# Twenty-six matmuls with unread results in two waits of TensorE

## The chip, the cores and the metric

The kernel runs on one core of one Trainium2 chip, in one launch. The metric is the device time in microseconds (us). The median of three runs before the change is 799.12 us.

## What is computed

Two layers on x of shape (4, 1024, 128), each with an attention part and a feed-forward part, all in float32. The change lies in the first layer, between the end of its attention and the start of its mixture of experts:

```python
x = x + _L0_attn_ref(_layernorm(x), Wq, bq, Wk, bk, Wv, bv, Wo, bo)   # 16 heads, causal, ALiBi
x = x + _L0_ffn_ref(_layernorm(x), Wr, br, W1, b1, W2, b2)           # 8 experts
x = x + _L1_attn_ref(_layernorm(x), Wq, Wk)                          # softmax(tanh(scores)) @ x
x = x + _L1_ffn_ref(_layernorm(x), weight, disha)
```

The feed-forward part of the first layer is a router and eight experts:

```python
logits = x @ Wr + br
gate = max(softmax(logits)); idx = argmax(logits)      # one expert per token
pos = cumsum(one_hot(idx)) over all 4096 tokens        # position in the expert's queue
gate = gate * (pos < 512)                              # each expert takes its first tokens only
out = gate * (relu((gate * x) @ W1[idx] + b1[idx]) @ W2[idx] + b2[idx])
```

## The kernel before

The program is two blocks. The first holds the attention of the first layer; its unnormalised weighted sums and the softmax denominators go to DRAM, and at its end the last batch of them is loaded back. The second block, `later_stages`, does the rest. It works on 32 tiles of 128 tokens, in 8 chunks of 4 tiles. Every engine has its own list of instructions, which it works off in the order in which the code writes them, and the engines meet at semaphores; there is no planner in this block.

TensorE's list in the second block begins with two products of weights into `psFold` (lines 1226 and 1227). Then `pe.wait_ge(rden_ready, B)` waits until VectorE has inverted the last denominators (line 1024), which wait for their DMA. `reciprocals(j)` (line 1195) spreads the inverted denominators of chunk j over the partitions, one matmul of 128x128 by 128x512 float. VectorE multiplies them with the weighted sums (`divide`, line 1030), TensorE multiplies with Wo (`project`, line 1203, 4 matmuls), and VectorE adds the result to the residual (`add`, line 1039) and takes statistics (line 1042). Two of the chunks are under way at a time. The layer norm ends in `apply` on VectorE (line 1066) or ScalarE (line 1353), and then TensorE transposes a chunk (`turned`, line 1215) and computes its logits (`logits`, line 1222, 4 matmuls of 8 columns).

Behind the last logits VectorE alone forms maximum, one-hot choice and, after three matmuls for counts (lines 1248 to 1250), positions and gates (lines 1111 to 1124). TensorE waits for the first gated chunk (`xg_ready`, line 1253), transposes it (`gated_columns`, line 1258), makes the one-hot rows (`one_hot_rows`, line 1264), with ScalarE's copies behind each (lines 1377, 1381, 1382). Then the loop over 8 chunks x 8 experts begins: `expert_in` (lines 1273 and 1274), ScalarE's Relu (line 1390), `expert_out` (line 1282), with the second layer's steps of earlier chunks set between them by a fixed table.

Every float matmul shows in the trace as two matmul records and two weight loads, a transpose as one of each.

PSUM areas that matter: `psLg` is half a bank pair, 512 columns, of which the logits of all tiles fill the first 256; `psT2[0]` holds the transposed chunks with even numbers, of which the last is read before the logits end. `ident` is the 128x128 identity, `sel` a 0/1 array of 128 x 8 x 128; both are constants in SBUF.

Of the kernel before, what the change touches and what calls it, by code (L numbers as in the profile page):

```python
# [19 lines left out]
CW = CH * P  # L20
# [861 lines left out]
def later_stages(nc, ctx, sb, sem, w, shared, out):  # L882

    x_res, ot, den, ident, half_pow, half, banks = (
        shared[k] for k in ("x_res", "ot", "den", "ident", "half_pow", "half", "banks"))
    wts_in, o_in, xb_ready, rden_ready, n_later, identb = (
        shared[k] for k in ("wts_in", "o_in", "xb_ready", "rden_ready", "n_later", "identb"))
    wo, wr, brb, rank, sel, incl, same, less = (
        w[k] for k in ("wo", "wr", "brb", "rank", "sel", "incl", "same", "less"))
# [56 lines left out]
    psRb, psProj, psT2, psLg = [half[0], half[1]], [banks[0], banks[1]], [half[2], banks[2]], half[3]  # L946
# [241 lines left out]
    def _(pe):  # L1188
        pe.wait_ge(wts_in, 16 * n_later)

        def reciprocals(j):

            if j >= 2:
                pe.wait_ge(at_ready, j - 1)
            nc.tensor.matmul(psRb[j % 2], sel[:, j, :], den[:, :, :].rearrange("p s q -> p (s q)"),
                             start=True, stop=True).then_inc(rb_psum, 1)
# [29 lines left out]
        nc.tensor.matmul(psFold[:, 0:P], w1q[:, :], w1k[:, :], start=True, stop=True)  # L1226
        nc.tensor.transpose(psFold[:, P:2 * P], wf[:, :], ident[:, :]).then_inc(fold_psum, 1)

        pe.wait_ge(rden_ready, B)
        reciprocals(0)  # L1230
        for j in range(CHUNKS):
# [16 lines left out]
        nc.tensor.matmul(psZ[0][:, 0:TILES * E], incl[:, :], flat, start=True, stop=True)  # L1248
        nc.tensor.matmul(psZ[0][:, TILES * E:2 * TILES * E], same[:, :], flat, start=True, stop=True)
        nc.tensor.matmul(psY[:, 0:TILES * E], less[:, :], flat, start=True, stop=True).then_inc(cnt_psum, 1)  # L1250

        def gated_columns(j):
            pe.wait_ge(xg_ready, j + 1)
            pe.wait_ge(fold_ready, 1)
            if j >= 1:
                pe.wait_ge(hott_ready, 2 * j)
            for i in range(CH):
                last = nc.tensor.transpose(psG[:, P * i:P * i + P], xg[:, j % 2, i, :], ident[:, :])
            last.then_inc(g_psum, 1)
# [34 lines left out]
        for n, (expert, due) in enumerate(slots()):  # L1294
            for name, j in due:
# [10 lines left out]
                if name == "s":  # L1306
                    pe.wait_ge(ut_ready, j + 1)
                    for i in range(CH):
                        last = nc.tensor.matmul(psS[:, P * i:P * i + P], xt3[:, P * i:P * i + P], ut[:, P * i:P * i + P],
                                                start=True, stop=True)  # L1310
                    last.then_inc(s_psum, 1)
                if name == "mix":
# [4 lines left out]
                    for i in range(CH):  # L1317
                        c0 = (i % 2) * (CW // 2)
                        last = nc.tensor.matmul(psMix[i // 2][:, c0:c0 + D + 1], ee[:, i, :], xe[:, j % 2, i, 0:D + 1],  # L1319
                                                start=True, stop=True)  # L1320
# [129 lines left out]
```

## Time and profile before

| | before |
|---|---|
| median of 3 runs | 799.12 us (798.9 to 801.77) |
| profiled execution, its own time | 797.04 us |
| its span, first to last instruction | 795.3 us |
| TensorE matmul busy | 662.6 us (83%) |
| VectorE busy | 515.1 us (65%) |
| ScalarE busy | 448.7 us (56%) |
| GpSimd busy | 153.8 us (19%) |
| mean granted TensorE clock | 0.921 of full |

The profile is of one execution. PE is TensorE's matmuls, PEld its weight loads, DVE VectorE, ACT ScalarE, POOL GpSimd. "L1195" is line 1195 of the kernel. The granted clock is 1.00 at 2.4 GHz and 0.50 at 1.2 GHz. A row of the timeline gives start, time, engine, line, operation, written and read tiles, shapes and count, and in brackets how long the engine had been idle and what released it.

### The profile page before, as it was taken

The numbers are of one execution on the slowest core, as the hardware profiler recorded it, in microseconds if no ns is written. First come the engines' busy times: TensorE is split into PE (matmuls) and PEld (weight loads), VectorE is DVE, ScalarE is ACT, GpSimd is POOL, SyncE is SP. The second block draws the span as 40 slices with busy tenths as digits, with TensorE's granted clock in tenths as the row PEclk, the third lists the DMA queues.
The fourth block names the chain that finished last, engine by engine and source line by source line (L and its number), as shares of the span: only waits on it lengthen the run. The fifth ranks groups of instructions, "written<-read, shape, count | busy, mean of one in ns | idle before, by whom it ended". The sixth has DMA issues, their size and how long they took to land.

```text
span 795.3 us, 14721 instructions
## 1 busy us (share of the span) xinstructions
PE 662.6 (83%) x5478; PEld 315.9 (40%) x5478; DVE 515.1 (65%) x1024; ACT 448.7 (56%) x765; POOL 153.8 (19%) x245
## 2 busy tenths in 40 slices
PE   3656988999989899889899885765799999999953
PEld 2431333333323233333333220455356666666643
DVE  5999788998888888889788830574221345333443
ACT  2950777788777887778777884032234443344310
POOL 2660122212221222212451221030000011010110
PEclk9995899999999999999999998685699999999965
DMA  6494645422212341332203000100000000000001
GB/s 157 133 200 122 160 109 139 107 46 49 52 34 48 72 76 36 75 72 50 50 7 77 6 10 10 28 1 0 1 0 1 10 6 14 14 14 6 9 13 27
DMA packets 49806, 40.58 MB, mean 51 GB/s; under 512 B 9772, under 2 KB 44724, under 8 KB 49724
## 3 DMA queue, kind: packets, MB, share of 16 engines
q1 hardware_dynamic: 43576, 37.22, 20.2%
q10 hardware_dynamic: 6160, 2.43, 1.3%
q8 instruction: 44, 0.72, 0.4%
q14 instruction: 26, 0.21, 0.1%
HBM read 22.32 MB, written 17.04 MB: 49 GB/s over the span
## 4 chain that ended last, share of the span: by engine, by line
PE 62%; DVE 19%; ACT 6%; issue 6%; POOL 3%; DMA 2%; SPq 0%; POOLq 0%; DVEq 0%; ACTq 0%
PE sums L756 15%; DVE neg_max L783 10%; PE ring L735 10%; PE ring L1282 9%; PE ring L1273 8%; PE bank L707 5%; ACT probs L804 5%; PE ring L1274 3%; PE bank L701 2%; DVE probs L506 2%; PE ring L1286 1%; PE bank L1319 1%; PE bank L1222 1%; PE bank L1330 1%; PE ring L718 1%
## 5 line engine op out<-in xcount | busy, mean ns | idle before, releaser
L783 DVE TENSOR_REDUCE neg_max<-bank 128x2 f32<-128x1024 f32 (+2 forms) x320 | 342.8, 1115 | 60.9 <-PE bank L707 58.8
L804 ACT ACTIVATE probs<-ring 128x512 f32<-128x512 f32 (+4 forms) x481 | 301.8, 681 | 79.8 <-PE ring L735 66.8
L735 PE MATMUL ring<-q_operand,k_operand 56*128 56x512 bf16 (+3 forms) x768 | 164.3, 333 | 18.2 <-ACT probs L804 14.5
L756 PE MATMUL sums<-probs,v_all 128*9 128x512 f32 (+3 forms) x1536 | 162.4, 495 | 2.7 <-POOL probs L837 2.1
L707 PE MATMUL bank<-k_operand,q_operand 54*128 54x512 bf16 (+3 forms) x768 | 144.5, 338 | 7.0 <-DVE v_all L514 5.3
L837 POOL TENSOR_SCALAR_AFFINE_SELECT probs<-probs 128x512 f32<-128x512 f32 x128 | 80.2, 635 | 215.6 <-ACT probs L804 214.7
L735 PEld LDWEIGHTS ring<-q_operand,k_operand 56*128 56x128 bf16 x768 | 50.2, 94 | 152.6 <-ACT probs L804 110.5
L1390 ACT ACTIVATE hid<-ring,b1c 128x512 f32<-128x512 f32 x64 | 44.0, 687 | 81.9 <-PE ring L1274 81.7
L701 PE MATMUL bank<-masks 64*128 64x128 bf16 (+2 forms) x768 | 71.9, 224 | 5.2 <-DVE neg_max L783 4.9
L1282 PE MATMUL ring<-w,hid 128*128 128x128 f32 x512 | 74.9, 290 | 0.0
L1273 PE MATMUL ring<-xgt,w 128*128 128x512 f32 x128 | 69.0, 621 | 1.2 <-ACT noth L1382 1.2
L1282 PEld LDWEIGHTS ring<-w,hid 128*128 128x128 f32 x512 | 62.8, 193 | 14.5 <-issue 12.9
L991 POOL TENSOR_TENSOR rs<-ve,half_pow 128x4 f32<-128x4 f32 x16 | 16.1, 1007 | 233.1 <-DVE ve L1011 233.1
L707 PEld LDWEIGHTS bank<-k_operand,q_operand 54*128 54x128 bf16 x768 | 46.1, 97 | 24.5 <-DVE neg_max L783 14.8
L701 PEld LDWEIGHTS bank<-masks 64*128 64x128 bf16 x768 | 36.7, 95 | 37.9 <-DVE neg_max L783 25.4
L1143 DVE SCALAR_TENSOR_TENSOR x_res<-ring,gate,x_res 128x128 f32<-128x128 f32 x32 | 9.0, 344 | 58.8 <-PE ring L1286 58.8
L756 PEld LDWEIGHTS sums<-probs,v_all 128*9 128x9 f32 x1536 | 23.2, 88 | 53.5 <-issue 39.8
L1179 DVE TENSOR_TENSOR res<-x_res,bank 128x512 f32<-128x512 f32 x8 | 5.5, 688 | 54.2 <-PE bank L1330 54.2
L718 PE MATMUL ring<-identb,max_parts 128*32 128x128 bf16 x32 | 7.1, 221 | 24.7 <-POOL max_parts L854 23.5
L1274 PEld LDWEIGHTS ring<-noth,big 8*128 8x128 bf16 x64 | 5.8, 91 | 50.0 <-issue 50.0
L1024 DVE RECIPROCAL denominators<-denominators 128x128 f32<-128x128 f32 x1 | 1.0, 952 | 37.3 <-DMA denominators<-weighted_sums 37.3
L1274 PE MATMUL ring<-noth,big 8*128 8x512 bf16 x64 | 25.1, 392 | 0.0
(156 smaller groups left out, 654.8 us busy)
## 6 DMA issues: line engine op xcount, KB each, us to landing
q_operand<-q_rows SPq DMA_DIRECT2D x64, 96.0 KB, 3.4
k_operand<-k_rows SPq DMA_DIRECT2D x32, 192.0 KB, 4.0
q_rows<-qk_parts SPq DMA_DIRECT2D x36, 128.0 KB, 2.4
k_rows<-qk_parts SPq DMA_DIRECT2D x36, 128.0 KB, 2.4
weighted_sums<-osum SPq DMA_DIRECT2D x128, 18.0 KB
sums_in<-in_L_attn_x SPq DMA_DIRECT2D x4, 512.0 KB, 7.3
q_operand<-max_rows_sb SPq DMA_DIRECT2D x128, 2.0 KB
sums_in<-weighted_sums SPq DMA_DIRECT2D x4, 512.0 KB
```

Of the source, the lines that this page charges most:

```text
L701: nc.tensor.matmul(ends, masks[rows, 0, a, :], masks[rows, 1, a:a + 1, 64 * a:P].to_broadcast([64, len(pairs), P - 64 * a]), start=a == 0, ...
L707: last = nc.tensor.matmul(ps[:, h, w * j:w * j + w], q_op[rows, buf, t // CH, p, P * (t % CH):P * (t % CH) + P], k_op[rows, buf, p, CW * k ...
L735: last = nc.tensor.matmul(psS[:, bank, w * j:w * j + w], k_op[rows, buf, p, P * kb:P * kb + P], q_op[rows, buf, c, p, q0:q0 + w], start=Tr ...
L756: last = nc.tensor.matmul(psO[32 * i:32 * i + HD + 1, q0:q0 + w], v_all[:, n, kb, i, :], probs[:, u % NPROBS, i // 2, i % 2, 0:w], start=u ...
L783: nc.vector.tensor_reduce(neg_max[:, n % 2, slot, kc, :, pairs[0]:pairs[-1] + 1, t % CH], src, AX.X, ALU.max, negate=True).then_inc(a_read, 1)
L804: nc.scalar.activation(dst, src, ACT.Exp).then_inc(ring_read, 1)
L837: nc.gpsimd.affine_select(out=tri, in_=tri, compare_op=ALU.is_ge, fill=0.0, base=0, pattern=[[0, GH], [1, P]], channel_multiplier=-1).then ...
L991: nc.gpsimd.tensor_tensor(rs[:, :], ve[:, :], half_pow[:, 0:CH], ALU.pow).then_inc(pw_ready, 1)
L1273: nc.tensor.matmul(psZ[n % 2], w1[:, e, :], xgt[:, j % 2, :], start=True, stop=False)
L1274: nc.tensor.matmul(psZ[n % 2], big[:, e, :], noth[:, j % 2, :], start=False, stop=True).then_inc(z_psum, 1)
L1282: nc.tensor.matmul(psY[:, P * i:P * i + P], hid[:, n % 3, P * i:P * i + P], w2[:, e, :], start=(e == 0 and i == 0), stop=False, skip_group ...
L1390: nc.scalar.activation(hid[:, n % 3, :], psZ[n % 2], ACT.Relu, bias=b1c[:, e:e + 1]).then_inc(hid_ready, 1)
```

## The change

A helper writes n matmuls of 128x128 by 128x256 float into the upper half of a PSUM area that nobody reads afterwards. Ten are written between the two products of weights and the wait for the reciprocals, sixteen between the three matmuls for the counts and the wait for the first gated chunk. They wait for nothing and signal nothing. Nothing else is changed.

```diff
@@ -1226,6 +1226,12 @@
         nc.tensor.matmul(psFold[:, 0:P], w1q[:, :], w1k[:, :], start=True, stop=True)
         nc.tensor.transpose(psFold[:, P:2 * P], wf[:, :], ident[:, :]).then_inc(fold_psum, 1)
 
+        def idle_work(bank, n):
+
+            for _ in range(n):
+                nc.tensor.matmul(bank[:, CW // 2:], ident[:, :], sel[:, 0:2, :].rearrange("p c m -> p (c m)"), start=True, stop=True)
+
+        idle_work(psLg, 10)
         pe.wait_ge(rden_ready, B)
         reciprocals(0)
         for j in range(CHUNKS):
@@ -1248,6 +1254,7 @@
         nc.tensor.matmul(psZ[0][:, 0:TILES * E], incl[:, :], flat, start=True, stop=True)
         nc.tensor.matmul(psZ[0][:, TILES * E:2 * TILES * E], same[:, :], flat, start=True, stop=True)
         nc.tensor.matmul(psY[:, 0:TILES * E], less[:, :], flat, start=True, stop=True).then_inc(cnt_psum, 1)
+        idle_work(psT2[0], 16)
 
         def gated_columns(j):
             pe.wait_ge(xg_ready, j + 1)
```

## Rows read from the trace of the kernel before

**Rows 1.** The page, part 4: shares of the chain by engine

```profile
PE 62%; DVE 19%; ACT 6%; issue 6%; POOL 3%; DMA 2%; SPq 0%; POOLq 0%; DVEq 0%; ACTq 0%
```

**Rows 2.** Window: width, busy of PE, PEld, DVE, ACT, POOL, granted clock, DMA

```profile
600.00:750.00 150.00, 150.00 (x821) 95.14 (x820) 61.77 (x282) 58.49 (x95) 12.08 (x12) 1.00 0.04 10
```

**Rows 3.** Chain in order of time, first wait: start, us, what

```profile
496.00 6.60 DMA denominators<-weighted_sums
...
503.64 3.78 PE bank L1195 x4
...
509.17 0.70 DVE x_res L1039
```

**Rows 4.** Timeline around the first wait

```profile
497.84 0.42 PE L1227 MATMUL sums<-ident,wf 128*128 128x128 f32 x1
...
505.75 0.69 DVE L1030 TENSOR_TENSOR at<-sums_in,bank 128x512 f32<-128x512 f32 x1 [2.17 <-PE bank L1195]
...
510.15 1.05 PE L1203 MATMUL ring<-wo,at 128*128 128x128 f32 x8
...
511.04 1.02 PE L1195 MATMUL bank<-denominators,sel 128*128 128x512 f32 x2
```

**Rows 5.** Timeline at the end of the attention

```profile
486.06 0.81 PE L735 MATMUL ring<-q_operand,k_operand 56*128 56x384 bf16 x3 [1.26 <-ACT probs L804]
```

**Rows 6.** Windows of one microsecond at the changes of the clock

```profile
489.00:490.00 1.00, 0.77 (x13) 0.19 (x9) 0.00 (x0) 0.78 (x2) 0.22 (x1) 0.91 0.00 0
...
496.00:497.00 1.00, 0.00 (x0) 0.00 (x0) 0.00 (x0) 0.00 (x0) 0.00 (x0) 0.50 0.25 49
...
509.00:510.00 1.00, 1.00 (x3) 0.45 (x3) 0.80 (x2) 0.00 (x0) 0.00 (x0) 0.67 0.00 0
...
523.00:524.00 1.00, 0.00 (x0) 0.00 (x0) 0.96 (x4) 0.96 (x3) 0.00 (x0) 0.66 0.00 0
...
530.00:531.00 1.00, 1.00 (x10) 1.00 (x10) 0.75 (x5) 0.03 (x1) 0.00 (x0) 0.93 0.08 16
...
536.00:537.00 1.00, 1.00 (x11) 1.00 (x11) 0.86 (x6) 0.46 (x1) 0.03 (x1) 0.98 0.00 0
```

**Rows 7.** Chain in order of time, second wait

```profile
560.66 1.10 PE sums L1258 x4
561.84 0.59 ACT xgt L1377
562.48 0.60 PE sums L1264 x4
...
564.31 2.04 PE ring L1273 x2
```

**Rows 8.** Timeline around the second wait and in the loop

```profile
552.47 0.42 PE L1250 MATMUL ring<-hotb,less 128*128 128x256 bf16 x1
...
571.17 1.02 PE L1273 MATMUL ring<-xgt,w 128*128 128x512 f32 x2
...
572.44 1.16 PE L1282 MATMUL ring<-w,hid 128*128 128x128 f32 x8
...
575.70 0.60 PE L1258 MATMUL sums<-ident,xg 128*128 128x128 f32 x4
...
578.50 0.39 PE L1264 MATMUL sums<-identb,hotb 128*8 128x128 bf16 x4
```

**Rows 9.** Timeline, PE only: transposes and logits, at either clock, and two pauses

```profile
524.02 1.12 PE L1215 MATMUL bank<-ident,xn 128*128 128x128 f32 x4 [3.76 <-ACT xn L1353]
...
535.19 0.66 PE L1215 MATMUL ring<-ident,xn 128*128 128x128 f32 x4 [2.36 <-DVE xn L1066]
535.68 0.96 PE L1222 MATMUL bank<-wr,xt 128*128 128x8 f32 x8
...
536.96 1.70 PE L1222 MATMUL bank<-wr,xt 128*128 128x8 f32 x8
538.52 1.09 PE L1215 MATMUL ring<-ident,xn 128*128 128x128 f32 x4
```

## Prediction

> **What bounds the kernel now.** I read the shares of the chain that ended last first [rows 1]: TensorE (PE) holds 62% of it, VectorE (DVE) 19%. The reader is to see that a microsecond taken off or put on PE's work is not at once a microsecond of the kernel; it depends on the stretch. The second view is the window from 600 to 750 us [rows 2]: PE is busy in all 150.00 us at the full clock. So whatever arrives earlier or later at the start of the expert loop moves the end by the same amount, and the question is only what the two edits do between 498 and 575 us.
>
> The third view is the chain in order of time around the first wait [rows 3]. The last denominators land at 502.6 us, VectorE inverts them, and at 503.64 the first broadcasting matmuls (line 1195) start; the first sum onto the residual (line 1039) starts at 509.17, 5.53 us later. The fourth is the chain around the second wait [rows 7]: 560.66 gated columns, 561.84 their copy, 562.48 one-hot rows, 564.31 the first expert.
>
> The fifth view is the granted clock by microseconds [rows 6]. It has two levels: 1.00 (2.4 GHz) and 0.50 (1.2 GHz). It falls within 496 to 497 us, after PE has done nothing since about 492, and is at 1.2 GHz over the whole first wait. It rises within 509 to 510, 6 us after PE began to work without a break at 503.64. It falls again within 523 to 524 (PE had stood still for the 3.76 us up to 524.02 [rows 9]), rises within 530 to 531 and falls at the end of 536 to 537; the 2.04 us of the first expert's line 1273 at 564.31 and the 1.02 us of the third's at 571.17 show that the next rise comes some 6.8 us after 564.31 [rows 7, 8]. So both places that the change touches are followed by 6 to 7 us of PE work on the path at half clock. That is what the edit can win.
>
> **What one added matmul costs.** Its stationary operand is 128x128 float, its moving one 128 x 256 float. The nearest rows are those with 512 columns: four records, that is two matmuls, take 3.78 us at 1.2 GHz [rows 3], 1.89 us each, of which the first weight load is some 0.2; and one (two records) takes 1.02 us at 2.4 GHz with its tail [rows 4], 0.86 when the next follows. Half the columns give 0.85 us at 1.2 GHz and 0.43 at 2.4. Ten take 8.5 or 4.25 us; sixteen take 13.6 or 6.8. Nothing is added on other engines and no semaphore is, and nobody reads the two PSUM areas. The cost is only where PE is still at it when the wanted operand arrives: the queue is in order, and behind the ten stand `reciprocals(0)` and everything after it, behind the sixteen `gated_columns(0)`.
>
> **When the clock rises.** The trace before shows no such stretch in the waits, so I take the delay from the nearest rises. PE worked from 486.06 and had 2.4 GHz at about 489.1 (3.1 us) [rows 5, 6]; from 503.64 to about 509.7 (6.0); from 564.31 to 571.1 (6.8). The ends are 3.1 and 6.8, and I take 5.0, the middle, because the three fall on both sides of it. With a delay r, the ten end at start + 4.25 + r/2, and the sixteen at start + 6.8 + r/2. The Trainium skill ("TensorE: Matmul & The Clock Gate", Part 1) says that the throttled state is the default and that activity releases it, and in the same part that the number of slow matmuls varies between runs of one kernel; the spread of 3.1 to 6.8 us in this trace agrees with the second. The same part puts the ramp at under 1% of a typical span and advises against fitting to one count; by that the change could give no more than some 8 us here, which is above my sum and leaves it as it is.
>
> **First edit, ten matmuls.** PE's last work before the wait is the transpose of line 1227 at 497.84, done at about 498.2 [rows 4]. So the ten end at E = 498.2 + 4.25 + 2.5 = 504.95, which is 1.3 us later than 503.64 (0.4 to 2.2 for the ends of r). From there it runs at 2.4 GHz: line 1195 1.0 us, VectorE's product (line 1030) 0.69 with handovers of 0.1 each side, meanwhile the second line 1195, so PE goes on at E + 2.0, line 1203 1.05, and line 1039 starts at E + 3.1 [rows 4]. That is 508.05 in place of 509.17: **1.1 us gained** (2.1 to 0.2). Afterwards PE's pair of 1.05 + 1.02 us per chunk and VectorE's own work set the pace as before, so the gain stays 1.1 and grows no further.
>
> **Second edit, sixteen matmuls.** They start behind line 1250, at 552.9 [rows 8], and end at 552.9 + 6.8 + 2.5 = 562.2, 1.5 us after 560.66 (0.6 to 2.4). The VectorE chain of counts and gates is untouched and hides the rest of them; were it shorter, all of it would be late. Then at 2.4 GHz line 1258 takes 0.60 in place of 1.10 and line 1264 0.39 in place of 0.60 [rows 7, 8]: 0.7 back. ScalarE's copies between them stay. The first expert starts 0.8 us late (0.1 early to 1.7 late). From its start to the third expert's it was 6.86 us (564.31 to 571.17); at 2.4 GHz two of lines 1273 and 1274 at 1.27 each (571.17 to 572.44) and one line 1282 at up to 1.16 make 3.6 [rows 8]. That is 3.25 for this execution, where the slow stretch was the longest of the trace; for the middle delay I take 5.0/6.8 of it, 2.4. Net **1.6 us gained**.
>
> **The sum.** 1.1 + 1.6 = 2.7 us. The profiled execution's own time is 797.04 us (span 795.3 and 1.7 around it); with its own long slow stretch it would be 1.1 + 3.25 - 0.8 = 3.55 shorter, 793.5. But the median of the runs shown is 799.12, 2.1 above the profiled one, and the runs reach from 798.9 to 801.77; a clock that rises and falls at other moments is my guess for that, and no row shows it. I set the change against the median with the middle delays: 799.12 - 2.7 = **796.4**. Its own range is 794.3 (r = 3.1 at both) to 798.3.
>
> **The rivals.**
> *The clock falls again in the pauses behind the second edit.* Between the end of the sixteen and the first expert PE stands still for 0.65 us (copy of the gated columns) and 1.25 us (copies of the one-hot rows) out of 2.9. Against: 2 us of pauses are less than the 3.76 around the fall at 523 [rows 6, 9]. For: the fall at 536.98 came with PE at work, after a pause of only 2.36 us that ended at 535.19 [rows 9], so short pauses suffice sometimes. Then the experts start at 1.2 GHz as before, 0.8 us later: +1.1 - 0.8 = 0.3 us gained, 798.8. [...]
>
> *The added matmuls do not raise the clock* (slower than before). The place is the same in both waits. For: from 536.96 on PE works on transposes and logits with hardly a break, and yet at 1.2 GHz to the end of them [rows 9]. Against: that stretch is made of matmuls with 8 columns, and the stretch that did rise at 509.7 was 512-column and 128-column float matmuls with the same weights' shape [rows 3, 4]. Price: the ten end at 498.2 + 8.5 = 506.7, 3.1 late; the sixteen at 552.9 + 13.6 = 566.5, 5.8 late; 799.12 + 8.9 = 808.0. It decides from a delay of about 7.2 us on: there the first edit is at E + 3.1 = 509.2, no gain.
>
> *The gain of the first edit is swallowed or multiplied between 524 and 549.* Moving PE's work by 1.1 us moves its pauses too, and there the clock is at 2.4 GHz only from 530 to 537 [rows 6]. A chunk's logits (line 1222) take 1.70 us at 1.2 GHz and 0.96 at 2.4 [rows 9], its transposes 1.1 and 0.6: 1.25 per chunk. Three chunks more at half clock cost 3.7 and leave 799.12 - 2.7 + 3.7 = 800.1; two more at full clock give 796.4 - 2.5 = 793.9.
>
> **How the numbers follow.** Forecast 0.52; clock falls again, 798.8: 0.27; never rises, 808: 0.08; middle zone worse, 800.1: 0.07; better, 793.9: 0.06. Half a per cent (4.0 us, below 795.1 and above 803.1) is about what a measurement of this kernel can tell from no change. Faster by over that: the fast end of the forecast (0.10) and the better middle zone (0.06), 0.16. Slower: the 808 case and 0.02 for a delay between, 0.10. Same: 0.74. The range 793.8 to 801.2 holds all but the 808 case and the ends of the others.
>
> **What would show it.** After the change: the granted clock rises within 501 to 505 and again within 556 to 560; the added matmuls show 0.85 us first and 0.43 later; the first line 1195 starts at 504 to 506 and yet line 1039 before 509.17; line 1258 starts at 561 to 563, and the first line 1273 takes 1.0 us rather than 2.0. If that line takes 2.0, the clock fell in the pauses. If line 1195 starts after 506.5, it never rose. The prediction is wrong if the clock over 524 to 549 differs by more than the two edits do.

## The result and the profile after

The kernel after the change takes 793.27 us in the median of 22 runs (789.46 to 797.07), the kernel before beside it 796.68 us (22 runs). The ratio is 0.9952 with a 95% interval of 0.9934 to 0.9971: 3.8 us, between 2.3 and 5.3. It is a ratio of means, while the medians are 3.4 us apart; one of the 22 runs before took 964.29 us and is left out of it, the others lie between 792.10 and 801.77. The forecast said 2.7 us gained, but put the time at 796.4 us with a range that began at 793.8, half a microsecond above the measured median.

The page of the profiled execution after, first line and busy times:

```profile
span 792.9 us, 14825 instructions
PE 675.0 (85%) x5530; PEld 325.9 (41%) x5530; DVE 515.0 (65%) x1024; ACT 448.9 (57%) x765; POOL 153.6 (19%) x245
```

PE is busy 12.4 us longer than before and has 52 more records (26 matmuls), and the kernel is still shorter; the other engines' busy times are within 0.2 us of before. PE's timeline after the change, both waits (lines after the first wait stand 6 or 7 further down than before: 1265 is 1258, 1271 is 1264, 1280 is 1273):

```profile
497.89 0.42 PE L1227 MATMUL sums<-ident,wf 128*128 128x128 f32 x1
498.10 6.26 PE L1232 MATMUL bank<-sel,ident 128*128 128x256 f32 x20
504.20 1.88 PE L1195 MATMUL bank<-denominators,sel 128*128 128x512 f32 x4
506.01 1.16 PE L1203 MATMUL ring<-wo,at 128*128 128x128 f32 x8
...
550.72 8.16 PE L1232 MATMUL bank<-sel,ident 128*128 128x256 f32 x32
558.71 0.61 PE L1265 MATMUL sums<-ident,xg 128*128 128x128 f32 x4
560.05 0.39 PE L1271 MATMUL sums<-identb,hotb 128*8 128x128 bf16 x4 [0.73 <-ACT xgt L1384]
561.69 1.10 PE L1280 MATMUL ring<-xgt,w 128*128 128x512 f32 x2 [1.24 <-ACT noth L1389]
562.72 0.38 PE L1281 MATMUL ring<-noth,big 8*128 8x512 bf16 x1
563.03 1.99 PE L1280 MATMUL ring<-xgt,w 128*128 128x512 f32 x2
...
570.83 1.02 PE L1280 MATMUL ring<-xgt,w 128*128 128x512 f32 x2
```

The ten took 6.1 us from their start to that of line 1195, and ended 0.9 us after the denominators were inverted; the four records of line 1195 then took 1.88 us where they had taken 3.78 [rows 3]. The sixteen ended just as the gated chunk was ready, the first expert ran at the full clock (1.10 us against 2.04 [rows 7]), and the second did not (1.99). The windows of one microsecond show why; their columns are those of [rows 6], the granted clock is the value in front of the last two:

```profile
501.00:502.00 1.00, 1.00 (x4) 0.80 (x4) 0.00 (x0) 0.00 (x0) 0.00 (x0) 0.65 0.21 31
...
552.00:553.00 1.00, 1.00 (x4) 0.82 (x3) 0.93 (x5) 0.00 (x0) 0.00 (x0) 0.55 0.00 0
...
563.00:564.00 1.00, 1.00 (x3) 0.42 (x2) 0.00 (x0) 0.69 (x1) 0.00 (x0) 0.57 0.00 0
...
569.00:570.00 1.00, 1.00 (x3) 0.36 (x3) 0.00 (x0) 0.16 (x1) 0.00 (x0) 0.51 0.00 0
```

It rose at 501.7, 3.6 us into the ten, and at 552.9, 2.2 us into the sixteen; it fell again at about 563.1, behind the two pauses of 0.7 and 1.2 us, and came back at 570. In this execution the second edit behaves as in the prediction's first rival. For the first line 1039, which stood at 509.17 us in [rows 3], the chain in order of time now has

```profile
507.20 0.70 DVE x_res L1039
```

which is 1.97 us earlier, with line 1226 at the same time as before within 0.05 us.

**Stages.** Single executions of one kernel differ by several microseconds in the attention, ahead of the change. So for the rest of this text every profile is divided at four instructions of its own timeline: S1 runs from the start of line 1226 to the start of the first line 1039; S2 from there to the first matmul for the counts (1248 before); S3 from there to the first matmul of the fourth expert of the first chunk (573.44 in the trace before). For before that is 11.89, 42.90 and 21.37 us, for after 9.87, 42.90 and 20.73. S2 is 42.87 to 42.95 in each of the 15 profiles in which nothing was added to it. From the fourth expert to the end it takes 221.8 to 222.0 us in 13 of the 15 profiles in which nothing was added there, so what is won ahead of the fourth expert reaches the end in full, as the prediction assumed.

### The profile page after: what moved, and what is told of

It is laid out like the page before. It is cut to its first block and busy times, and to the rows that moved or that the text cites. A ratio compares the mean times of both kernels' runs of the same rounds, so it can differ in the third digit from the quotient of the medians.

```text
span 792.9 us, 14825 instructions
## 1 busy us (share of the span) xinstructions
PE 675.0 (85%) x5530; PEld 325.9 (41%) x5530; DVE 515.0 (65%) x1024; ACT 448.9 (57%) x765; POOL 153.6 (19%) x245
```

## The experiments

Each was timed against the kernel before on the same chip, apart from three single profiled runs.

**One edit alone, twice.** The diffs leave out one line each:

```diff
-        idle_work(psT2[0], 16)
```

> Only the ten matmuls ahead of the reciprocals. Theory (the added work raises TensorE's clock ahead of the wanted work): 1.1 to 2.0 us under the kernel before, with line 1039 starting some 3 us after the first line 1195 instead of 5.5. Rival (the gain lies in the second wait): no difference from before.

> Only the ten. By the traces so far 1.2 to 2.0 us under before. If the run before this one (2 us) was chance, no difference.

Ratios 0.9974 (0.9945 to 1.0003) and 0.9979 (0.9953 to 1.0005), medians 796.61 and 795.14. S1 10.69 and 9.67, S3 22.18 and 20.11 as before. By the times alone neither is clear of no difference; both are near 2 us.

```diff
-        idle_work(psLg, 10)
```

> Only the sixteen matmuls ahead of the first gated chunk. Theory: 1.6 us under before where the clock stays up, 0.8 us over it in executions in which the clock falls again in the two pauses of the one-hot rows; the two edits add up to the whole change (3.4 us). Rival (the gain lies in the first wait): no difference, or up to 0.8 us slower.

> Only the sixteen. If the edits add, it is 2 to 3 us under before and 1.2 to 2 us over the whole change. If its 5.8 us of the run before was real, the first edit costs something in the second's presence, and this kernel is again under the whole change.

Ratios 0.9927 (0.9899 to 0.9955) and 0.9944 (0.9919 to 0.9968), medians 791.99 and 792.86. S1 11.39 and 11.68, as before; S3 18.38 and 18.43. The rival that all the gain lies in the first wait falls. But this kernel was forecast 1.6 us under before and above the whole change, and by its ratios it is 5.8 and 4.5 us under before, as much as the change itself shows (3.8). Part of that lies elsewhere: in both of its profiles the clock also rose once for 3.4 us near the end of the kernel, which no other kernel without added matmuls there shows, and from the fourth expert to the end they take 220.9 and 221.0 us, 0.9 less than the others. Why it rose there was not tried. That the first edit adds something on top of the second is therefore read from the stages and not from the times. PE's timeline of the first of the two shows an execution in which the clock stayed up through the pauses (here 1264 and 1279 are 1258 and 1273 of before):

```profile
549.21 8.99 PE L1232 MATMUL bank<-sel,ident 128*128 128x256 f32 x32
558.03 0.60 PE L1264 MATMUL sums<-ident,xg 128*128 128x128 f32 x4
...
560.99 1.10 PE L1279 MATMUL ring<-xgt,w 128*128 128x512 f32 x2 [1.25 <-ACT noth L1388]
...
562.34 1.12 PE L1279 MATMUL ring<-xgt,w 128*128 128x512 f32 x2
...
564.70 1.02 PE L1279 MATMUL ring<-xgt,w 128*128 128x512 f32 x2
```

The sixteen are 0.85 us late (9.44 us from the counts to line 1264, 8.59 before), and the third expert's matmul comes 3.71 us after the first's where it took 6.86 before. The prediction had 3.6 for it; its terms, 1.27 twice and 1.16, add up to 3.70.

**Is it the clock, or only that PE is occupied?** The added matmuls stream 8 columns instead of 256; the counts of them fill the same waits.

```diff
-                nc.tensor.matmul(bank[:, CW // 2:], ident[:, :], sel[:, 0:2, :].rearrange("p c m -> p (c m)"), start=True, stop=True)
+                nc.tensor.matmul(bank[:, CW // 2:CW // 2 + E], ident[:, :], sel[:, 0, 0:E], start=True, stop=True)
-        idle_work(psLg, 10)
+        idle_work(psLg, 12)
-        idle_work(psT2[0], 16)
+        idle_work(psT2[0], 18)
```

> The added matmuls with 8 columns instead of 256, 12 and 18 of them, so that TensorE is occupied for 5.1 and 7.7 us but hardly streams columns. Theory that streamed work raises the clock: it stays at 1.2 GHz, as over the logits of before, and the time is that of the kernel before within 1 us. Rival (any occupation of TensorE does it): some 3 us under before, as the whole change.

Ratio 0.9990 (0.9957 to 1.0023). PE's timeline:

```profile
495.62 5.13 PE L1232 MATMUL bank<-sel,ident 128*128 128x8 f32 x24
501.16 3.78 PE L1195 MATMUL bank<-denominators,sel 128*128 128x512 f32 x4 [0.41 <-DVE denominators L1024]
...
550.24 7.69 PE L1232 MATMUL bank<-sel,ident 128*128 128x8 f32 x36
558.21 1.09 PE L1265 MATMUL sums<-ident,xg 128*128 128x128 f32 x4 [0.28 <-issue]
...
561.86 2.05 PE L1280 MATMUL ring<-xgt,w 128*128 128x512 f32 x2 [1.24 <-ACT noth L1389]
```

By the profile PE was occupied for 5.1 and 7.7 us without a break, and the work behind it still ran at 1.2 GHz: 3.78, 1.09 and 2.05 us, within 0.01 the values of before [rows 3, 7]. S1 is 11.83, S3 21.41. The same kind of matmul with 8 columns, where the weight loads took 5.03 of the 5.13 us and 7.59 of the 7.69, did not raise the clock; with 256 columns it did.

**Twice the matmuls.**

```diff
-        idle_work(psLg, 10)
+        idle_work(psLg, 20)
-        idle_work(psT2[0], 16)
+        idle_work(psT2[0], 32)
```

> Twice the added matmuls, 20 and 32, in the two waits. By the working of the prediction the second half runs at 2.4 GHz and is late in full: 10 x 0.43 = 4.3 us in the first wait and 16 x 0.43 = 6.9 in the second, so 11.2 us over the change and 7.8 over before. If TensorE were waiting at the end of the added work in the change, the lateness would be less than that by this spare time.

Ratio 1.0077 (1.0053 to 1.0101), 803.74 us: 6.2 us over before, where 7.8 were expected. PE's timeline:

```profile
497.19 11.35 PE L1232 MATMUL bank<-sel,ident 128*128 128x256 f32 x40
508.37 1.88 PE L1195 MATMUL bank<-denominators,sel 128*128 128x512 f32 x4
...
554.86 15.02 PE L1232 MATMUL bank<-sel,ident 128*128 128x256 f32 x64
569.71 0.60 PE L1265 MATMUL sums<-ident,xg 128*128 128x128 f32 x4
...
574.02 2.07 PE L1280 MATMUL ring<-xgt,w 128*128 128x512 f32 x2
```

The twenty put line 1195 5.96 us behind the inverted denominators, where the ten put it 0.6 to 1.8 behind: the lateness that was priced at 0.43 us a matmul is there in full (4.3 priced, 4.2 to 5.4 seen). The gated columns start 15.46 us after the counts, 6.5 to 6.9 more than in the change. The 2.07 us of the expert at 574.02 show that the clock fell behind the pauses here as well. This execution, 805.41 us, is among the longer of ten (800.3 to 806.7).

**The pauses ahead of the first expert filled, twice.**

```diff
         gated_columns(0)
+        idle_work(psT2[0], 1)
         one_hot_rows(0)
+        idle_work(psT2[0], 2)
         expert_in(0)
```

> The change, and one more added matmul in the pause ahead of the one-hot rows and two in the pause ahead of the first expert. Theory (the clock falls again in these pauses in part of the executions, and the experts start at 1.2 GHz): the granted clock is 1.00 through the first experts, and the median is 1 to 2.5 us under that of the change, 4.5 to 6 under before. Rival (the fall is rare, or the fill is late): like the change, within 0.5 us.

> The change with the two pauses filled. If the clock falls in the pauses in about half of the executions of the change, and never here, the median is some 1.5 us under that of the whole change, 5 to 6 under before, and the stretch from the counts to the fourth expert takes 17.6 us again. If the fall in the profiled execution of the change was a rare one, the same as the whole change.

Ratios 0.9918 (0.9893 to 0.9943) and 0.9933 (0.9904 to 0.9962). PE's timeline of the first:

```profile
560.73 0.60 PE L1232 MATMUL bank<-sel,ident 128*128 128x256 f32 x2
561.62 0.39 PE L1271 MATMUL sums<-identb,hotb 128*8 128x128 bf16 x4 [0.29 <-ACT xgt L1386]
561.94 1.13 PE L1232 MATMUL bank<-sel,ident 128*128 128x256 f32 x4
563.25 1.10 PE L1280 MATMUL ring<-xgt,w 128*128 128x512 f32 x2 [0.18 <-ACT noth L1391]
...
564.60 1.12 PE L1280 MATMUL ring<-xgt,w 128*128 128x512 f32 x2
```

The pauses shrink to 0.29 and 0.18 us, the experts behind them run at full clock, and S3 is 17.56 in both profiles (17.23 in three later kernels that have this edit too). But the times did not show the 1 to 2.5 us under the change that were expected: the intervals overlap those of the change, and beside the change on the same chip this kernel has a median of 792.91 us against 792.12.

**How often does the clock fall in the pauses?** The change again beside its parts, then three single profiled runs.

> The whole change once more, beside its parts on the same chip. If the stages add as the traces so far show: 2.0 us gained between the first product of weights and line 1039, and 0.6 or 3 to 4 us between the counts and the fourth expert, according to whether the clock falls in the pauses; 3 to 5 us under before in the median, and under each part alone.

Ratio 0.9916 (0.9885 to 0.9946), 792.12 us. S1 10.57, S3 17.90: the clock stayed up. Its parts alone had 795.14 and 792.86 beside it, so the sixteen alone are only 0.7 us behind the whole, where 1.2 to 2 were expected.

> The kernel before, once more with a profile. If the stage lengths are what they were in the first profile: 11.9 us from the first product of weights to line 1039 and 20 to 22 from the counts to the fourth expert, while the attention ahead of them may differ by several us; the whole from the first product of weights to the end 298 us.

> The change once more with a profile. First stage 9.7 to 10.7 us; from the counts to the fourth expert 17.9 to 19.2 us if the clock stays up in the pauses, 20.7 if it falls. If falls are as rare as in the traces so far (one in five), it stays up.

> The same as the look before it: one in five to fall, by the traces so far; if both looks fall, the prediction's rival with 0.27 was nearer the half.

The kernel before: S1 10.38, S3 22.22, and 297.4 us from line 1226 to the end (298.0 in the first profile). The expectation for S1 was missed: the clock rose at about 507.7 there, only 3.4 us after line 1195 began. The change: S1 10.53 and 9.85, S3 17.88 and 20.73. In the second of these runs of the change the clock fell as in the first profile:

```profile
553.51 8.14 PE L1232 MATMUL bank<-sel,ident 128*128 128x256 f32 x32
561.49 0.63 PE L1265 MATMUL sums<-ident,xg 128*128 128x128 f32 x4
...
565.83 2.03 PE L1280 MATMUL ring<-xgt,w 128*128 128x512 f32 x2
```

So the clock fell in two of four profiles of the change, and in two of the seven profiles of all kernels with sixteen added matmuls and open pauses. In both the sixteen were not late at all (8.59 and 8.61 us from counts to gated columns); the five that were late (8.95 to 10.20) stayed up. The doubled kernel was 6.9 us late and fell, so lateness alone does not decide it. One reading sorts all eight: how long after the start of the added matmuls the clock rose. It was 2.1 to 2.2 us in the three that fell, and 2.9 to 5.4 in the five that stayed up. The two profiles with filled pauses rose after 2.1 and 2.2 us too, were not late either, and did not fall; against the two that fell their S3 is 3.2 us shorter. That filling the pauses kept the clock up is thus borne out by two profiles; why an early rise goes with a fall stays open.

The two runs of the change also show where executions differ apart from that. ScalarE makes the 28th of its 32 copies of sums at

```profile
441.43 0.59 ACT L817 COPY osum<-sums 128x512 f32<-128x512 f32 x1
```

in the first run and, by the same view, at

```profile
444.64 0.59 ACT L817 COPY osum<-sums 128x512 f32<-128x512 f32 x1
```

in the second: 3.2 us between two executions of the same code, over 50 us ahead of the change. They are as far apart at 138 us already, and keep that distance while both have the full clock, from 150 to 450 us; over 50 to 100 us the granted clock is 0.73 in the first and 0.69 in the second, over 450 to 500 it is 0.90 and 0.84. Line 1226 starts at 494.88 and 500.14, and over all profiles of this study between 494.30 and 500.33, though nothing ahead of it was ever changed.

**The other waits of PE.** On top of the filled pauses, the waits between the first projection and the counts:

```diff
+            if j == 5:
+                idle_work(psLg, 3)
             project(j)
             if j == 5:
+                idle_work(psLg, 7)
                 turned(0)
...
             if j + 1 < CHUNKS:
+                if j == 2:
+                    idle_work(psLg, 5)
                 turned(j + 1)
             logits(j)
...
+        idle_work(psT2[0], 7)
         pe.wait_ge(hot_ready, 1)
```

> The change with the two pauses filled, and added matmuls in TensorE's other waits of the same stage: 3 ahead of the sixth projection, 7 ahead of the first transposes, 5 ahead of the fourth, 7 ahead of the counts. Theory (the clock state over the logits is what is still lost): it stays at 2.4 GHz from about 502 us on, five chunks of logits and transposes are 1.25 us shorter each where TensorE sets the pace, 4 to 6 us under the pauses-filled kernel. Rival (the 8-column logits let the clock fall whatever stands in the pauses): the logits keep their 1.7 us and the kernel gains under 1.5 us.

Ratio 0.9893 (0.9862 to 0.9924), 789.74 us. S2 fell from 42.9 to 40.74: 2.2 us, between the 4 to 6 that were expected and the under 1.5 of the rival. The clock stayed up to 537.7 and then fell, behind a pause of 1.4 us ahead of the seventh transposes:

```profile
537.42 0.92 PE L1215 MATMUL bank<-ident,xn 128*128 128x128 f32 x4 [1.42 <-ACT xn L1368]
```

The last run has four more matmuls in this pause. It is the kernel with everything filled, below, and has the tail of the next experiment too:

```diff
                 if j == 2:
                     idle_work(psLg, 5)
+                if j == 5:
+                    idle_work(psLg, 4)
                 turned(j + 1)
```

> Everything filled, and four more added matmuls ahead of the seventh transposes, where the clock fell in the kernel with everything filled (PE stood 1.4 us there). Theory (that pause lets it fall): the clock stays at 2.4 GHz to the counts, the last logits take 0.96 us per chunk instead of 1.71, and 2 us come off. Rival (the 8-column logits themselves let it fall): it falls there again, and nothing or up to 1 us of lateness comes of it.

Ratio 0.9790 (0.9758 to 0.9821), 781.05 us, S2 37.71. Both theories have a part. Filling the pause was worth 2.9 us of S2 (40.65 with everything else filled), and behind it the clock fell all the same, three microseconds later, at 540.7, with PE at work in every one of them. The last logits and the windows of this kernel:

```profile
538.65 0.63 PE L1215 MATMUL ring<-ident,xn 128*128 128x128 f32 x4
539.12 2.08 PE L1222 MATMUL bank<-wr,xt 128*128 128x8 f32 x16
```

```profile
539.00:540.00 1.00, 1.00 (x12) 1.00 (x10) 0.00 (x0) 0.58 (x1) 0.00 (x0) 1.00 0.00 0
540.00:541.00 1.00, 1.00 (x9) 1.00 (x9) 0.00 (x0) 0.00 (x0) 0.00 (x0) 0.84 0.00 0
```

**The tail.** The change, and PE's waits behind the last expert:

```diff
             for name, j in due:
+                if n >= CHUNKS * E:
+                    idle_work(psZ[0], TAIL.get((name, j), 0))
```

with 12 ahead of the last but one `mix`, 3 ahead of the last, 12 ahead of the last `t4`, and one each ahead of the last `u`, `s` and the last two `f`.

> The change, and added matmuls in TensorE's pauses behind the last expert (12 ahead of the last but one mix, 12 ahead of the last transposes, 7 in between). Theory: the clock stays up in the last 35 us, where before every line took 2.1 us instead of 1.05; eight such pieces on the path give 6 to 8 us under the change. Rival (VectorE and ScalarE set the end and TensorE's speed is hidden): under 2 us.

Ratio 0.9895 (0.9865 to 0.9925), 789.86 us. From the last bias matmul of the experts to the end it takes 32.2 us, where before took 37.2 to 37.3. That is 5 us, a little under the expectation. The last two `mix` and the last product each take 1.16 us now instead of 2.1; the last but one `mix`, before and now:

```profile
765.38 2.09 PE L1319 MATMUL bank<-xe,ee 128*128 128x129 f32 x8 [6.17 <-DVE ee L1157]
```

```profile
762.96 1.16 PE L1329 MATMUL bank<-xe,ee 128*128 128x129 f32 x8 [0.79 <-DVE ee L1157]
```

**All of it.**

> All of it together. If the gains add: 10 to 16 us under before's median; if the stages only hand waiting time on: no better than the better of the two parts.

Ratio 0.9832 (0.9802 to 0.9862), 785.09 us, S1 10.30, S2 40.65, S3 17.23 and 32.1 us of tail: the gains add (12.4 us by the medians, of the 10 to 16 expected). With the four matmuls ahead of the seventh transposes it is the 0.9790 above, the fastest kernel of the study, with nothing of the computation left out and 86 added matmuls.

## Why the prediction was wrong, and what of it was right

**The mechanism and the sign** were right. The clock rises in both waits, the added work is a little late in the first and at times in the second, and the delay is more than won back. The narrow matmuls show that the clock is what matters: the same waits filled without raising it gave nothing in either stage.

**The absolute time** failed at the step that set the sum against the median of three runs. 796.4 was 799.12 less 2.7; over 22 runs the kernel before has a median of 796.68, 2.4 us lower, and in later comparisons 796.76 to 798.44. Of the 3.1 us between 796.4 and the measured 793.27, this step makes 2.4, and the sum of the gains, 2.7 where the medians show 3.4, the other 0.7. The prediction noticed that the profiled execution (797.04) lay 2.1 us under the three and took the three all the same. The guess that a different history of the clock lies behind it fits: among the 22 runs of the change the longer ones have the lower mean granted clock (correlation -0.91, for example 790.88 us with 0.935 and 796.72 with 0.918), and the two single runs of the change differ by 3.2 us within the attention. That the clock is the cause there was not tried. A spread of 792 to 802 us in the kernel before is wider than the whole forecast range; the range should have carried the uncertainty of a median of three. Its inner ends, 794.3 and 798.3, come to 794.5 and 798.2 by the prediction's own terms, which changes nothing here.

**First edit:** predicted 1.1 us. Mean S1 without the ten is 11.34 (11.89, 10.38, 11.39, 11.68), with them 10.17 in twelve profiles: 1.2. Line 1195 started 0.5 to 1.7 us late (predicted 1.3, bounds 0.4 to 2.2), and from line 1195 to line 1039 it took 3.0 us (predicted E + 3.1). The gain is 2.0 only between the two first profiles, 11.89 and 9.87, each on its own side of the mean. That 1.1 was met this closely is partly luck, for two errors cancel: the prediction worked from a profile 0.5 us above the mean, and it took 5.0 us until the clock rises, where it rose 3.2 to 5.2 us after the ten began, 4.2 in the mean, which makes 0.4 us less of lateness.

**Second edit:** predicted 1.6 us. Mean S3 without the sixteen is 21.47 (four profiles), with them and open pauses 19.03 (seven): 2.4. This term was mis-sized, by two steps. The delay before the clock rises was 2.2 to 5.4 us in this wait, 3.3 in the mean of the seven, where 5.0 had been taken and 3.1 was the lower bound; so the gated columns were 0 to 1.6 us late, 0.6 in the mean, and not 1.5. And the gain on the first experts was scaled by 5.0/6.8, though the slow stretch of before is about as long in every profile: S3 is 20.1 to 22.2 without the sixteen, and 21.37 was no outlier. In the five profiles in which the clock stayed up, the case that the 1.6 was worked out for, the gain is 3.1 us.

**The rivals.** The fall in the pauses had 0.27 and came in two of seven profiles. Its price was wrong: S3 is 0.7 us shorter than before, not 0.8 longer. The two executions that fell are those without lateness, and in the traced line the first expert still ran at full clock (1.10 us). With that, even a fall leaves the whole change about 2 us ahead. The rival in which the clock never rises (0.08) did not come. Its price of a matmul was right: in the trace after, the added matmuls start 0.85 us apart at 1.2 GHz and 0.43 at 2.4. The middle stage as a place of loss or gain (0.13) is out: S2 is 42.9 us whatever happened ahead of it. That the same pauses and 8-column logits set its clock each time is a reading of the profiles and was not tested apart.

## What to carry to other kernels

The two waits filled here had TensorE idle for 5.4 and 7.8 us and were followed by float matmuls on the path. Such waits are worth filling with matmuls that stream many columns, in a number whose time, part of it at 1.2 GHz (6.1 us for the ten, 8.0 for the sixteen), is not far above the wait; each one too many costs its full time at 2.4 GHz on the path. Look for the next pauses behind the place where the clock was raised, which the profiles of this case show to matter though the times could not, and do not forget the end of the kernel: here the two given waits brought 0.5% and all of them together 2.1%. And when single runs of a kernel spread by 1%, divide profiles into stages at instructions that both kernels have, rather than compare spans.

## What was not expected of the hardware

- PE at work in every microsecond did not hold the clock: in a stretch of transposes and 8-column float logits from 537.4 us on it fell from 2.4 to 1.2 GHz at 540.7 us, and 7.7 us of 8-column float matmuls without a break did not raise it. 256-column float matmuls raised it after 2.1 to 5.4 us in these two waits.
- Behind two pauses of 0.7 and 1.2 us within 3 us the clock fell in two of seven profiles, and not in the other five.
- Executions of the same code differ by 6 us (494.30 to 500.33) in when they reach the same instruction; of the 5.3 us between the two that were compared, 3.3 are there by 138 us.
